# Softmax reciprocals by way of DRAM instead of TensorE, and one score tile sooner, in the first attention of a gated two-layer block

## What is computed

```python
kv = jnp.concatenate([context, latents], axis=1)      # 512 + 256 = 768 keys
q = (latents @ Wq).reshape(bsz, q_len, HEADS, HEAD_DIM).transpose(0, 2, 1, 3)
k = (kv @ Wk).reshape(bsz, kv_len, KV_HEADS, HEAD_DIM).transpose(0, 2, 1, 3)
v = (kv @ Wv).reshape(bsz, kv_len, KV_HEADS, HEAD_DIM).transpose(0, 2, 1, 3)
q = rms_norm(q, q_norm_w)
k = rms_norm(k, k_norm_w)
scores = jnp.einsum('bhgqd,bhkd->bhgqk', qg, k) * scale
probs = jax.nn.softmax(scores.astype(jnp.float32), axis=-1).astype(q.dtype)
out = jnp.einsum('bhgqk,bhkd->bhgqd', probs, v)
...
return out @ Wo
```

## Time and profile before

| | |
|---|---|
| median of 3 runs | 1024.17 us (1023.63 to 1025.63) |
| profiled execution | 1025.66 us |
| its span | 1023.8 us, mean granted TensorE clock 0.99 |
| PE (TensorE matmuls) busy | 982.4 us, 96% |
| DVE busy | 628.1 us, 61% |
| ACT busy | 501.9 us, 49% |
| POOL busy | 356.8 us, 35% |
| DMA traffic | 46.53 MB |

### The profile page before, as it was taken

One profiled execution on the slowest core, in us unless ns is written; L12 is line 12 of the kernel. 1 busy time (PEld: TensorE's weight loads), 2 busy tenths in 40 slices (PEclk: granted clock), 3 DMA queues, 4 the chain that ended last, 5 costly groups with the idle time before them and its releaser, 6 DMA issues. The chain is left out here.

```text
span 1023.8 us, 18226 instructions
## 1 busy us (share of the span) xinstructions
PE 982.4 (96%) x6748; PEld 846.9 (83%) x6748; DVE 628.1 (61%) x1102; ACT 501.9 (49%) x969; POOL 356.8 (35%) x244
## 2 busy tenths in 40 slices
PE   4999999999999999999999999999999999999996
PEld 3879989998998899899989989898977776666655
DVE  5567457556745754675566467556653865777746
ACT  4356337534743663464366346435624413656534
POOL 3335316233531623344163334423333530440033
PEclk9989999999999999999999999999999997999999
DMA  6011002001100210020011002000034207722001
GB/s 225 1 62 43 2 1 102 1 0 34 68 0 0 64 39 0 3 99 0 0 61 41 0 0 102 20 0 1 2 96 149 96 16 184 175 40 47 2 1 42
DMA packets 31460, 46.53 MB, mean 45 GB/s; under 512 B 3520, under 2 KB 15424, under 8 KB 31424
## 3 DMA queue, kind: packets, MB, share of 16 engines
q1 hardware_dynamic: 30848, 46.03, 15.1%
q10 hardware_dynamic: 576, 0.00, 0.0%
HBM read 41.83 MB, written 4.19 MB: 45 GB/s over the span
## 5 line engine op out<-in xcount | busy, mean ns | idle before, releaser
L438 DVE TENSOR_TENSOR ptL<-tbank,ptH 128x512 fp32r<-128x512 f32 x192 | 132.2, 688 | 82.9 <-ACT ptH L298 82.7
L298 ACT ACTIVATE ptH<-tbank 128x512 fp32r<-128x512 f32 x192 | 115.8, 603 | 91.2 <-PE tbank L550 90.6
L550 PE MATMUL tbank<-ident,probs 128*128 128x128 f32 x864 | 131.1, 276 | 5.3 <-DVE qTL L440 2.8
L324 ACT ACTIVATE probs<-score,negmax 128x768 f32<-128x768 f32 x128 | 115.7, 904 | 29.6 <-DVE negmax L451 29.6
L451 DVE TENSOR_REDUCE negmax<-score 128x1 f32<-128x768 f32 x128 | 118.8, 948 | 14.4 <-PE score L80 14.4
L78 PE MATMUL obank<-ptH,vH 128*128 128x256 f32 x384 | 121.4, 316 | 0.0
L409 DVE TENSOR_REDUCE sumsq<-probs 128x2 f32<-128x256 f32 (+1 forms) x80 | 42.1, 526 | 113.3 <-ACT probs L293 71.8
L550 PEld LDWEIGHTS tbank<-ident,probs 128*128 128x128 f32 x864 | 97.9, 140 | 14.5 <-DVE probs L417 3.0
L206 POOL TENSOR_TENSOR rnorm<-sumsq,neg_half 128x2 f32<-128x2 f32 (+1 forms) x80 | 72.0, 902 | 107.5 <-DVE sumsq L411 107.4
L80 PE MATMUL score<-wkvH,kvT_lo 128*128 128x256 f32 x384 | 108.7, 283 | 0.0
L79 PE MATMUL score<-wkvL,kvT_hi 128*128 128x256 f32 x384 | 108.7, 283 | 0.0
(11 more groups left out here) (272 smaller groups left out, 2301.8 us busy)
## 6 DMA issues: line engine op xcount, KB each, us to landing
wqo_stage<-in_wq SPq DMA_DIRECT2D x9, 1024.0 KB, 5.6
wqo_stage<-in_wo SPq DMA_DIRECT2D x8, 1024.0 KB, 5.1
wkv_stage<-in_wkv SPq DMA_DIRECT2D x9, 512.0 KB, 6.4
a_qS<-q_scratch SPq DMA_DIRECT2D x24, 128.0 KB, 4.9
ctx_stage<-in_ctxT SPq DMA_DIRECT2D x2, 1024.0 KB, 13.5
kS<-k_scratch SPq DMA_DIRECT2D x32, 64.0 KB, 3.2
q_scratch<-qpart SPq DMA_DIRECT2D x16, 128.0 KB, 1.9
wqo_stage<-in_down_w SPq DMA_DIRECT2D x3, 512.0 KB, 3.5
```

What stands on the lines that cost most here:

```text
L298: act.activation(out, tbank[c % 2][:], ACT.Copy, scale=scale).then_inc(t_hi, 1)
L324: act.activation(probs[:, m % NP, :], score[m % 2][:, 0:SKV], ACT.Exp, bias=negmax[:, m:m + 1], accum_out=rsum[:, m:m + 1]).then_inc(s_exp, 1)
L438: i = dve.tensor_tensor(out, tbank[c % 2][:], f32(hi), ALU.subtract)
L550: i = pe.transpose(tbank[c % 2][:, n * P:(n + 1) * P], block_in, S.ident[:])
```

## The change

TensorE's transposes of the factors go, and with them ACT's copies. After a head's reciprocals SP sends the four columns of `rsum` (128 values of 4 bytes each, one from each partition) to a row of a DRAM scratch, waits until they have landed, and reads the row of 512 values back to all 128 partitions of a new tile `factors`. DVE multiplies `obank` with `factors` into `o_norm`; it now waits for this read and, in ACT's place, for POOL to be done with the head before. SP's transfers stand behind the turn's weight loads, in the last turn between Wo and wkv1. DVE makes a head's reciprocals earlier in their unit, ahead of the second maximum, or in unit 7 of the blocks. In unit 0 TensorE does the scores of tile 2 ahead of the first transposes of probabilities and those of tile 3 behind them, and DVE takes tile 2's maximum ahead of the low part of block 0.

```diff
+    o_norm, factors = sb("o_norm", [P, ROWS], fp32), sb("factors", [P, ROWS], fp32)
+    r_dram = nc.dram_tensor("r_scratch", (GRP, ROWS), fp32, kind="Internal").ap()
+    r_out, r_in, o_normed = sem("r_out"), sem("r_in"), sem("o_normed")
...
-        if u % 2 == 1 and u >= 3:
-            order.append(("r", (u - 3) // 2))
...
                 S.load_wkv(sp, g + 1)
+                for h in range(GRP):
+                    spread_factors(g, h)
+
+            def spread_factors(g, h):
+
+                sp.wait_ge(r_inv, GRP * g + h + 1)
+                for n in range(RT):
+                    sp.dma_start(r_dram[h, n * P:(n + 1) * P].rearrange("(q a) -> q a", a=1),
+                                 rsum[:, 4 * h + n:4 * h + n + 1]).then_inc(r_out, 16)
+                sp.wait_ge(r_out, 16 * RT * (GRP * g + h + 1))
+                sp.dma_start(factors[:], r_dram[h].partition_broadcast(P)).then_inc(r_in, 16)
 
             def last():
                 sp.wait_ge(wq_split, NS * LAST + NS)
                 S.load_wo(sp, LAST)
+                for h in range(GRP):
+                    spread_factors(LAST, h)
...
-            def factors(g, h):
-                if h:
-                    act.wait_ge(o_lo, GRP * g + h)
-                hi(g, ("r", h), o_norm[:])
-
             def hi_o(g, h):
-                act.wait_ge(t_lo, TC * g + at["r", h] + 1)
+                act.wait_ge(o_normed, GRP * g + h + 1)
...
             def normalise_o(g, h):
-                c = at["r", h]
-                dve.wait_ge(t_hi, TC * g + c + 1)
+                dve.wait_ge(r_in, 16 * (GRP * g + h + 1))
                 dve.wait_ge(pe_pv, 24 * g + 2 * CH * (h + 1))
-                dve.tensor_tensor(o_norm[:], obank[h % 2][:], o_norm[:], ALU.mult).then_inc(t_lo, 1)
+                if h:
+                    dve.wait_ge(o_lo, GRP * g + h)
+                dve.tensor_tensor(o_norm[:], obank[h % 2][:], factors[:], ALU.mult).then_inc(o_normed, 1)
 
             def attend(g):
                 for u in range(U):
                     if u == 0:
                         lo_q(g, 1)
-                        lo(g, ("p", 0), ptL[:, 0, :], ptH[:, 0, :])
                     if u + 1 < U:
                         maximum(g, 2 * u + 2)
+                    if u == 0:
+                        lo(g, ("p", 0), ptL[:, 0, :], ptH[:, 0, :])
                     if u and u % 2 == 0 and u // 2 + 1 < GRP:
                         lo_q(g, u // 2 + 1)
                     if u % 2 == 1 and u >= 3:
                         normalise_o(g, (u - 3) // 2)
+                    if u % 2 == 1:
+                        reciprocals(g, u // 2)
                     if u + 1 < U:
                         maximum(g, 2 * u + 3)
                     for c in range(max(CH * u, 1), CH * u + CH):
                         lo(g, ("p", c), ptL[:, c % NPT, :], ptH[:, c % NPT, :])
-                    if u % 2 == 1:
-                        reciprocals(g, u // 2)
...
-            def transpose_factors(g, h):
-                pe.wait_ge(r_inv, GRP * g + h + 1)
-                transposes(g, ("r", h), [rsum[:, 4 * h + n:4 * h + n + 1].to_broadcast([P, P]) for n in range(4)])
-
-            def scores(g, u):
+            def scores(g, u, tiles=(0, 1)):
...
                     if u == 0:
+                        scores(g, 1, (0,))
                         transpose_probs(g, 0, 0)
-                    if u + 1 < U:
+                        scores(g, 1, (1,))
+                    elif u + 1 < U:
                         scores(g, u + 1)
```

More of the change, by code:

```diff
@@ L117, in attn0 @@
     oTH, oTL = sb("oTH", [P, GRP, ROWS], f32r), sb("oTL", [P, GRP, ROWS], f32r)
-    o_norm = sb("o_norm", [P, ROWS], fp32)
+    o_norm, factors = sb("o_norm", [P, ROWS], fp32), sb("factors", [P, ROWS], fp32)
+    r_dram = nc.dram_tensor("r_scratch", (GRP, ROWS), fp32, kind="Internal").ap()
+    r_out, r_in, o_normed = sem("r_out"), sem("r_in"), sem("o_normed")
     ss, rn = sb("sumsq", [P, 40], fp32), sb("rnorm", [P, 40], fp32)
@@ L132, in attn0 @@
             order.append(("q", u // 2 + 1))
-        if u % 2 == 1 and u >= 3:
-            order.append(("r", (u - 3) // 2))
         order += [("p", CH * u + j) for j in range(CH)]
-    order.append(("r", GRP - 1))
     at = {name: i for i, name in enumerate(order)}
@@ L332, in attend @@
                         hi_q(g, u // 2 + 1)
-                    if u % 2 == 1 and u >= 3:
-                        factors(g, (u - 3) // 2)
                     hi_p(g, CH * u)
@@ L352, in turn @@
                 evac_q(g + 1, 0)
-                factors(g, GRP - 1)
                 evac_q(g + 1, 1)
@@ L363, in last @@
                 attend(LAST)
-                factors(LAST, GRP - 1)
                 hi_o(LAST, GRP - 1)
@@ L571, in scores @@
                     pe.wait_ge(t_lo, TC * g + at["k", 1 + b] + 1)
-                for m in (2 * u, 2 * u + 1):
+                for m in (2 * u + t for t in tiles):
                     if u:
@@ L591, in times_v @@
                 if u % 2 == 0 and j == 0 and h >= 2:
-                    pe.wait_ge(t_lo, TC * g + at["r", h - 2] + 1)
+                    pe.wait_ge(o_normed, GRP * g + h - 1)
                 pe.wait_ge(t_lo, TC * g + at["p", c] + 1)
@@ L605, in attend @@
                         transpose_q(g, u // 2 + 1)
-                    if u % 2 == 1 and 3 <= u < U - 1:
-                        transpose_factors(g, (u - 3) // 2)
                     if u == 0:
+                        scores(g, 1, (0,))
                         transpose_probs(g, 0, 0)
-                    if u + 1 < U:
+                        scores(g, 1, (1,))
+                    elif u + 1 < U:
                         scores(g, u + 1)
@@ L614, in attend @@
                             times_v(g, u - 1, j)
-                            if j == 0:
-                                transpose_factors(g, (u - 3) // 2)
                         if u or j:
@@ L624, in finish_units @@
                     times_v(g, U - 1, j)
-                transpose_factors(g, GRP - 1)
             def output(g, t):
```

## The result

| | before | changed |
|---|---|---|
| median, us | 1024.9 (4 runs) | 1130.09 (4 runs, 1127.74 to 1134.76) |
| ratio to before | | 1.1033 (95%: 1.0992 to 1.1073) |
| span of the profiled execution, us | 1023.8 | 1125.7 |
| mean granted TensorE clock | 0.99 | 0.951 |

105 us more. The forecast was 1020.3, its range 1012 to 1031.

A forecast was written before the change was run, and what follows sets the result against it. TensorE was taken to set the pace (busy 99.15 of a hundred microseconds). Gain 18.7, head 0's stalls 13.3 and last turn's loss 1.5 gave -3.9 us, forecasting 1020.3 us, range 1012 to 1031.

The forecast's parts named there:

- it lands after 1.9: SP's column stores for each head: the fourth column lands 1.9 us after its issue, taken from stores of q_scratch.
- a chain of 5.8 us: Each head's transfers: issues 1.36, landing 1.9, wake-up 0.1 and spread read 2.4, 5.8 us in all.
- 5.8 fits, with over 3 us to spare: Heads 1 and 2: the transfers hide within DVE's spans of 11.3 and 9.5 us, less 0.44 in places.
- where I had 1.9: Head 0, behind the weight loads: TensorE stalls nearly 1.9 us in each of seven turns, 13.3 us in all.
- -18.7: Gain from removed transposes and the first unit: 2.67 us a turn over seven turns, 18.7 us.
- The value of the removal: TensorE's transposes of factors gone, 2.27 us a turn; with the first unit's 0.4, 2.67 a turn, 21.4 over eight.
- The first unit's 0.4 us a turn: Unit 0, tile 2's scores and maximum earlier: PE idles less ahead of tile 4, gaining 0.4 us a turn.
- The queue order: SP's queue at head 0: columns pass in order behind the weights, the last landing some 0.5 us after Wkv.
- Head 3 of the loop's turns hidden: Head 3's normalisation waits behind the next turn's first sum of squares, at no cost.
- The last turn's mechanism: Last turn: wkv1's load stands behind four spreads, POOL waits, the last head's products start 1.5 us later (0.6 to 4.0).
- (a): Rival: slow 4-byte column stores, 7 us per extra microsecond at head 0; about 1029, or past 1040 us; chance 0.24.
- the 9.6 us row: Evidence for the slow-column rival: an eight-byte fan-in of 1 KB landed after 9.6 us, at the start beside megabytes.

The follow-up runs named there:

- e1: Single transfers alone on SP, rest of the core idle, varying piece size and spacing; 128 neighbouring 4-byte pieces landed after 7.2 us, 64 or 512 bytes apart after 1.4.
- e8: Single transfers alone with pitches and sizes between, and a small store behind weight loads; pitch 16 showed no slowness, the store landed 0.15 us after Wkv.
- e13: Groups of stores alone on SP: four columns apart landed after 1.5 us each, four interleaved after 3.9; a just-stored row read in 3.9, again in 3.0.
- e5: Changed kernel with one store of 16-byte pieces per head in place of four, multiplication reading with a stride of four: 1040.95 us, ratio 1.0167 to the kernel before.
- e10: Changed kernel with four stores of 4-byte pieces, each column's pieces 16 bytes apart, the columns interleaved: 1125.44 us, ratio 1.1001 to the kernel before.
- e4: Changed kernel with head 0's spread ahead of the loads of Wq and Wkv in the loop's seven turns: 1123.65 us, ratio 1.0968 to the kernel before.
- e14: e2 with one extra DVE instruction of 2.56 us ahead of head 0's multiplication: 1033.19 us, ratio 1.0104 to the kernel before.
- e9: Changed kernel with one store per head and wkv1's load ahead of the last turn's spreads, head 0 still behind the weights: 1030.51 us, ratio 1.0069.
- e2: Changed kernel without its transfers, factors set to ones once: 1003.48 us, ratio 0.9786 to the kernel before.
- e6: Changed kernel with wkv1's load ahead of the spreads in the last turn, nothing else: 1139.34 us, ratio 1.111 to the kernel before.
- e12: e7 with the plain multiplication instead of the strided one, each factor going to another query than its own: 1004.54 us, ratio 0.981 to the kernel before.
- e15: e7 with a copy on ACT that puts the factors side by side, so DVE multiplies without a stride: 1005.25 us, ratio 0.9812 to the kernel before.
- e7: Changed kernel with one store per head, head 0's spread ahead of the weight loads and wkv1 ahead of the last turn's spreads: 1009.76 us, ratio 0.9865.

## Why the prediction was wrong

**The failed step: "it lands after 1.9".** I took a column's store from q_scratch's row, a store of large pieces, and made a chain of 5.8 us. It is 13.0: the four columns 8.7 instead of 3.3, the read 4.3 instead of 2.4. The cause of the first is shown: pieces that share a 16-byte word of DRAM (e1, e8, e13), and in the kernel one store of 16-byte pieces took 89 us off (e5), while four stores of 4-byte pieces into the same bytes left 85 of them (e10). The second is partly shown: a row just stored reads in 3.9 us, later in 3.0 (e13), with one of three rounds at 3.1; the rest I leave open.

**What hung on it.** "5.8 fits, with over 3 us to spare" was the step that let heads 1 and 2 cost nothing. With 13 us none of the spans of 9.5 to 11.3 holds it. PE's waits in the turn read, 11.5 us, are heads 0 and 2, and e4 shows head 1 behind them.

**A term that was missing.** Most waits of TensorE above 2 us are followed by some microseconds at the lower clock. I priced a stall at its length. By e14 it costs 1.7 times that for waits of 2.3 us (1.5 to 1.9 by the intervals). It isn't a fixed surcharge: in the changed kernel the clock stayed full behind two of the loop's seven waits at head 2 (3.19 and 3.55 us), and in e5 behind three of seven at head 0. Even the right stall would have made the forecast wrong: in e9 head 0 alone costs 3.0 us a turn where I had 1.9, and the sum -18.7 + 21 + 1.5 is +3.8, not -3.9.

**What was right.** The value of the removal, by the slot and not by the duration of the transposes: 21.4 us, measured 21.9 (e2). The first unit's 0.4 us a turn (0.6 measured, within its interval), and its sign: PE's waits for the exponential of tile 2 fell from 4.9 us in eight turns to 0.2. The queue order: small stores land 0.15 to 0.2 us after Wkv (e8, e5). The Trainium skill (DMA: Bandwidth & Descriptors, Queues, rings and completion order) says that each DMA engine takes the descriptors of a ring in order, and these rows agree with it. Head 3 of the loop's turns hidden. The last turn's mechanism, POOL caught behind wkv1, though not its size: PE waits 4.3 us for it in e5, whose chain is near the one I had assumed, against my 1.5, and 10.4 in the changed kernel.

**The rival.** (a) named the mechanism, the direction and even heads 1 and 2, and got 0.24, most of it for a microsecond or so. Its evidence, the 9.6 us row, was no witness of this effect: it is a load, and a load of 128 neighbouring 4-byte pieces landed after 2.0 us (e1). So the rival was right in its outcome, and what it went by says nothing of it. The Trainium skill's sentence on pieces under 512 B (DMA: Bandwidth & Descriptors, Specifications) speaks of the full rate; it pointed the right way, but the landing of these small stores has no step at 512 bytes: 16, 64 and 512 bytes a piece all land after 1.4 to 1.5 us (e1).

**Left open.** Why 16 partitions of 4-byte neighbours land in 1.3 us alone and eight such stores don't, what makes the collisions differ between programs (e6), which waits of TensorE lower the clock, and 2 to 3 us between e12 or e15 and e2, which lie inside the intervals.

## To carry to other kernels

A small transfer's price depends on where its pieces fall: before a column of single values goes to DRAM, see whether the values of a partition can lie side by side in one piece of 16 bytes or more, and whether another store writes the same word. Where a new transfer shares a queue with bulk loads, put it ahead of them or count their whole landing time. And where TensorE is the bound, a stall isn't paid by its length alone: look at the granted clock in the stretch behind it, in more than one turn.

## What the runs showed of the hardware that I had not expected

- A store of 128 neighbouring 4-byte pieces to DRAM lands after 7.2 us, with a pitch of 8 after 3.1, of 16 or more after 1.4; in SBUF neighbours cost nothing of this kind (1.9).
- The same collision between different stores: four interleaved columns are complete 7.1 to 7.6 us after the first issue, four columns apart after 3.4 to 4.3.
- A 2 KB row of one SBUF partition spread to 128 partitions takes 11.1 to 11.3 us, a 2 KB row in DRAM 3.0 to 4.8 with nothing else running, the most when it has just been stored.
- After a wait of 8.3 us TensorE ran at the lower clock level for some 5.4 us. After waits of 2.3 to 3.6 us it did so in most turns and not in others, with the same code and nearly the same wait.
- A DVE multiplication of 512 values a partition takes 1.09 us instead of 0.69 when one of its three operands is read with a stride of four (e7 and e12).
